# The residual of the second attention half added by TensorE, statistics and normalisation read from PSUM

## The chip, the cores and the metric

The kernel runs on one core of a Trainium2 chip. The metric is the device time of one execution in microseconds. Three runs of the kernel before gave 1319.53, 1314.14 and 1319.28 us, median 1319.28 us.

## The reference

A graph network with four layers runs over x of 1250 nodes by 512 features, with 40000 edges. Each layer first takes h = relu(layernorm(x)) and then adds its result to x. The change is in the second layer, an attention layer. Behind the attention itself, with o the attention's output after Wo, that layer computes:

```
x1 = layernorm(h + o) * ln1_g + ln1_b
f  = relu(x1 @ W1 + b1) @ W2 + b2          # 512 -> 256 -> 512
y  = layernorm(x1 + f) * ln2_g + ln2_b
x  = x + y
h  = relu(layernorm(x))                    # input of the third layer
M  = h @ Wm + bm                           # 512 -> 256, the third layer's messages
```

Only the step x1 + f and the statistics and normalisation that read it are changed. All arithmetic of this part is in 32-bit floats.

## The kernel before

The kernel is written by hand: each engine has its own instruction list, and semaphores order them. The nodes lie in ten tiles of 128 rows (the last has 98), and most stages are a loop over these tiles, spread over several engines. The order on each engine is the order of its list; nothing is rescheduled.

The stage that the change touches is called `l1b` in the code. Its work for tile t goes round like this.

- **TensorE** (`node_tiles`, L496 to L524). For tile t it writes one PSUM bank, t modulo 4. First comes a small 16-bit product with a row of ones, which lays down the bias (L511), and then two 32-bit products of 128 by 128 with 128 by 512 (L514). A 32-bit product is issued as two instructions, so L514 shows four MATMUL for a tile. From tile 4 on, it first waits until the bank's earlier tile is read (L504, semaphore `l1b_y`). After the product of tile t, from t = 6 on, it turns the tile t - 6 of the next layer's h with four transposes (L550, function `turn`), which wait until ScalarE has copied the turned tile two before out of PSUM. After the last tile, it computes the messages (L700, function `message`): eight MATMUL for a tile, four products in two instructions each. The first message waits for `l1b_y` of all ten tiles (L697), since the messages are written to banks 0 to 2, 4 and 5; for the weights `Wm` (L696), whose transfers SyncE issues once the products of all ten tiles are done (L374 to L377); and for the turned tile. Messages 0 to 3 run together behind turn 4, and then each turn is followed by one message, the last turn by two.
- **VectorE** (L1085 to L1104). In pass t it adds the residual to the bank and writes the sum to a buffer in SBUF (L1091, reading `H`, which holds x1), takes the statistics (L918, L919, L920), finishes mean and scale of the tile t - 1 (L925, L926), multiplies the normalised tile t - 2 with gamma (L1000), takes the statistics of the updated X of tile t - 3 (L918 to L920 again, reading X) and finishes the scale of tile t - 4 of X (L925, L926). A small instruction is followed by a wait for its own result where the next one reads it.
- **ScalarE** (`tail`, L1252 to L1267). In pass t: the square root of tile t (L1196), the normalisation of tile t - 1 in its SBUF buffer (L1242, semaphore `l1b_z`), the square root for X of tile t - 3, the relu of X of tile t - 4 into h (L1203), and the copy of the turned tile t - 6 out of PSUM (L1250).
- **GpSimd** (`shift_and_add`, L1372 to L1381). For each tile, it adds beta in the buffer (L1377) and adds the buffer to X (L1380).

The stage before it ends with the products of `x1 @ W1`, whose result ScalarE writes with a relu to SBUF (L1319). H of all ten tiles was complete before these products. Behind the messages VectorE adds their bias (L1109), and TensorE turns the edge-weight sums (L720) and goes on to the sums over edges (L736, L744).

Of the kernel before, what the change touches and what calls it, by code (L numbers as in the profile page):

```python
# [16 lines left out]
ACT = mybir.ActivationFunctionType  # L17
# [7 lines left out]
N, D, E = 1250, 512, 40000  # L25
T = -(-N // P)
KF = D // P
# [27 lines left out]
LAG = 6  # L55
# [41 lines left out]
def build(nc, A, out):  # L97
# [4 lines left out]
    with ExitStack() as ctx:  # L102
# [5 lines left out]
        def sem(name):  # L108
            if name not in sems:
                sems[name] = ctx.enter_context(nc.semaphore(name))  # L110
            return sems[name]
# [5 lines left out]
        H = sb("H", [P, T, D])  # L117
# [5 lines left out]
        stats = sb("stats", [P, 2, 6])  # L123
        mv = sb("mv", [P, 4, 2])
        rs = sb("rs", [P, 4, 2])
# [15 lines left out]
        PS = ctx.enter_context(nc.psum_tensor("PS", [P, 8 * BANK], F32))  # L141

        ident = K1[:, K_IDENT:K_IDENT + P]
# [9 lines left out]
        ybuf = R0[:, 0:4 * D].rearrange("p (s o) -> p s o", s=4)  # L153

        def bank(b, n=BANK):
            return PS[:, b * BANK:b * BANK + n]
# [55 lines left out]
        ybuf1 = R0[:, 5120:5120 + 4 * D].rearrange("p (s o) -> p s o", s=4)  # L212
# [19 lines left out]
        bias_parts = R0[0:BROWS, S0:S0 + D // 2].bitcast(BF16)  # L232
# [161 lines left out]
        def _(pe):  # L394
            mm = nc.tensor.matmul
# [98 lines left out]
                          "l0_h1_ps", "l0_h1_ev")  # L494

            def node_tiles(st, ks, lhs, rhs, width=D, turned=None, turned_width=KF, ready=None, then=None,  # L496
                           bias=None, banks=4, first=None, beside=None, lag=LAG, after=None):

                for t in range(T + (lag if turned else 0)):
                    if t < T:
                        if t >= banks:
                            pe.wait_ge(sem(st + "_y"), t - banks + 1)  # L504
                        if first:
                            first(t)
                        n = rows(t)
                        for part in range(len(ks)):
                            o = (t % banks) * BANK + part * width
                            if bias is not None:  # L510
                                mm(PS[0:n, o:o + width], ones_row[:, 0:n], bias, start=True, stop=False,  # L511
                                   skip_group_check=True)
                            for k in range(ks[part]):
                                i = mm(PS[0:n, o:o + width], lhs(part, k, t, n), rhs(part, k),  # L514
                                       start=k == 0 and bias is None, stop=k == ks[part] - 1, skip_group_check=True)
                        i.then_inc(sem(st + "_mm"), 1)
                        if beside:
                            beside(t)
                    if turned and t >= lag:
                        turn(st, t - lag, turned, turned_width, ready)  # L520
                    if then and t >= T:
                        then(t - lag)
                    if after and t > lag:
                        after(t - lag - 1)  # L524
# [167 lines left out]
            def message(t):  # L692

                n = rows(t)
                if t == 0:
                    pe.wait_ge(sem("l2_w_in"), 48)  # L696
                    pe.wait_ge(sem("l1b_y"), T)  # L697
                pe.wait_ge(sem("l1b_ht"), t + 1)
                for k in range(KF):
                    i = mm(PS[0:n, m_at(t):m_at(t) + 256], ht[:, k, t * P:t * P + n], wm[:, k, :], start=k == 0,  # L700
                           stop=k == KF - 1, skip_group_check=True)
                i.then_inc(sem("l2m_mm"), 1)

            def messages(i):
                for t in (range(0, i) if i == T - LAG else [i - 1]):
# [2 lines left out]

            pe.wait_ge(sem("l1_f1_ev"), 2)
            pe.wait_ge(sem("bias_parts"), BIAS_STEPS)  # L710
            node_tiles("l1b", [2], lambda q, k, t, n: f1t[:, k, t * P:t * P + n], lambda q, k: w2b[:, k, :],
                       turned=h_block, ready="l2_h", then=messages, bias=bias_parts)
            message(T - 1)

            def turn_sources(j, b0, done):
# [88 lines left out]
        def _(dve):  # L804
# [177 lines left out]
            def y_of(t, w=D, buf=ybuf):  # L982
                return buf[0:rows(t), t % 4, 0:w]
# [7 lines left out]
            def spread_of_y(name, t, w=D, buf=ybuf):  # L991
                spread_of(y_of(t, w, buf), rows(t), t % 4, name, stats, mv)
# [92 lines left out]
            for t in range(T + 4):  # L1085
                if t < T:
                    n = rows(t)
                    dve.wait_ge(sem("l1b_mm"), t + 1)
                    if t == 0:
                        dve.wait_ge(sem("l1_x1"), T)  # L1090
                    ve.tensor_tensor(y_of(t, D, ybuf1), bank(t % 4)[0:n], H[0:n, t, :], ALU.add).then_inc(sem("l1b_y"), 1)  # L1091
                    dve.wait_ge(sem("l1b_y"), t + 1)
                    spread_of_y("l1b_yn", t, D, ybuf1)
                if 1 <= t <= T:
                    scale_of_y("l1b_yn", t - 1)
                if 2 <= t < T + 2:
                    scaled("l1b", t - 2, bc1[:, 2, :], D, ybuf1)
                if 3 <= t < T + 3:
                    dve.wait_ge(sem("l1b_upd"), t - 2)
                    spread_of_x("l2_xn", t - 3)  # L1100
                if t >= 4:
                    scale_of_x("l2_xn", t - 4)
# [62 lines left out]
        def _(act):  # L1165
# [70 lines left out]
                for t in range((0, 3, 6, 9)[f], (3, 6, 9, T)[f]):  # L1236
                    lnc(t)

            def normed(st, t, w=D, buf=ybuf):
                n = rows(t)  # L1240
                act.wait_ge(sem(st + "_yn"), t + 1)
                sc.activation(buf[0:n, t % 4, 0:w], buf[0:n, t % 4, 0:w], ACT.Identity, bias=rs[0:n, t % 4, 1:2],  # L1242
                              scale=rs[0:n, t % 4, 0:1]).then_inc(sem(st + "_z"), 1)

            def turned(st, t, width=KF, dst=None):
# [3 lines left out]
                d = ht[:, :, t * P:t * P + n] if dst is None else dst[:, t * P:t * P + n]  # L1249
                sc.copy(d, src if dst is None else bank(6 + t % 2, n)).then_inc(sem(st + "_ht"), 1)  # L1250

            def tail(st, xn=None, done=None, width=KF, dst=None, w=D, buf=ybuf, beside=None, lag=LAG, after=None):  # L1252

                for t in range(T + lag + (1 if after else 0)):
                    if t < T:
                        root(st + "_yn", t, mv, rs)
                    if 1 <= t <= T:
                        normed(st, t - 1, w, buf)
                    if beside and t < T:
                        beside(t)  # L1260
                    if xn and 3 <= t < T + 3:
                        root(xn, t - 3, mv2, rs2)
                    if xn and 4 <= t < T + 4:
                        relu_rows(xn, done, rs2)(t - 4)
                    if lag <= t < T + lag:
                        turned(st, t - lag, width, dst)
                    if after and t > lag:  # L1267
                        after(t - lag - 1)
# [48 lines left out]
            for f in range(2):  # L1317
                act.wait_ge(sem("l1_f1_ps"), f + 1)
                sc.activation(f1t[:, f, 0:N], PS[:, 3 * f * BANK:3 * f * BANK + N], ACT.Relu,  # L1319
                              bias=bias_col[:, 4 + f:5 + f]).then_inc(sem("l1_f1_ev"), 1)  # L1320
            tail("l1b", "l2_xn", "l2_h", buf=ybuf1)


            act.wait_ge(sem("l1b_mm"), T)
# [129 lines left out]
```

## Time and profile before

| | |
|---|---|
| profiled execution | 1319.42 us |
| its span in the profile | 1317.2 us |
| median of three runs | 1319.28 us |
| TensorE matmul busy | 1155.9 us, 88% |
| VectorE busy | 630.0 us, 48% |
| ScalarE busy | 426.2 us, 32% |
| GpSimd busy | 142.6 us, 11% |
| granted TensorE clock, mean | 0.956 |

Times in the rows below are counted from the start of the span. Busy shares are means over stages that differ: the stage `l1b` with the messages behind it lies between 945.3 and 1002.0 us, and VectorE is busy in nearly all of its first 40 us. The granted clock is a share of the full 2.4 GHz; 0.50 is 1.2 GHz.

### The profile page before, as it was taken

To read this page: it belongs to the slowest core of one execution; us is meant where nothing else is said; L and a number is where in the kernel's file an instruction comes from. 1 tells how busy PE (TensorE), PEld (TensorE's weight loads), DVE (VectorE), ACT (ScalarE), POOL (GpSimd) and SP (SyncE) were. 2 spreads that over 40 slices of the span, in tenths; PEclk is the share of its full clock that TensorE was granted. 3 is DMA by queue.
4 is the path that set the end of the run, shared out by engine and by line. 5 is a ranking of instruction groups with operands and counts; after the bars stand their busy time and mean duration, and the time that the engine had idled before them with its cause. 6 is when DMAs were issued, how large, how long until landed. Compare 5 with 4: busy or idle time off the path is not lost.

```text
span 1317.2 us, 17306 instructions
## 1 busy us (share of the span) xinstructions
PE 1155.9 (88%) x5852; PEld 712.6 (54%) x5852; DVE 630.0 (48%) x1796; ACT 426.2 (32%) x711; POOL 142.6 (11%) x112
## 2 busy tenths in 40 slices
PE   1378877779999999979999999999868998799998
PEld 1134444445654445557777777764447556455543
DVE  6877877760007730056666666556394002610033
ACT  2401233320015440145555555543255003630000
POOL 0000000005560520000000000012172000200000
PEclk9997688779999999999999999999989999899999
DMA  4002477778783011000000000051010060000011
GB/s 145 0 0 59 132 199 211 202 203 298 257 271 124 0 32 48 17 1 1 1 2 1 2 1 1 1 187 75 0 33 0 0 227 0 1 32 0 0 40 38
DMA packets 67072, 93.78 MB, mean 71 GB/s; under 512 B 4857, under 2 KB 55872, under 8 KB 66998
## 3 DMA queue, kind: packets, MB, share of 16 engines
q1 hardware_dynamic: 66998, 92.78, 22.2%
q8 instruction: 48, 0.79, 0.3%
q14 instruction: 26, 0.21, 0.1%
HBM read 58.16 MB, written 34.60 MB: 70 GB/s over the span
## 4 chain that ended last, share of the span: by engine, by line
PE 71%; DVE 12%; DMA 7%; issue 4%; ACT 3%; SPq 2%; POOL 1%; DVEq 0%; ACTq 0%; POOLq 0%
PE PS L650 7%; PE PS L472 7%; PE PS L633 6%; PE PS L765 6%; PE PS L607 6%; PE PS L437 6%; DMA edge_parts<-X 6%; PE PS L514 5%; PE PS L799 5%; PE PS L578 5%; PE PS L736 3%; PE PS L744 3%; PE PS L487 3%; PE PS L568 2%; DVE R L1056 2%
## 5 line engine op out<-in xcount | busy, mean ns | idle before, releaser
L437 PE MATMUL PS<-HT,R 125*128 125x313 bf16 (+1 forms) x636 | 177.5, 414 | 64.0 <-DVE HT L947 26.4
L437 PEld LDWEIGHTS PS<-HT,R 125*128 x636 | 103.2, 172 | 139.0 <-issue 105.6
L1045 DVE CUSTOM_DVE_ANT_0 HT<-PS,CD 128x1250 f32<-128x1250 f32 (+1 forms) x80 | 116.4, 1455 | 55.4 <-issue 55.4
L633 PE MATMUL PS<-K,HT 128*128 128x128 f32 (+2 forms) x800 | 112.1, 279 | 15.3 <-DVE R L1056 14.5
L955 DVE TENSOR_SCALAR HT<-BC,HT 125x314 f16 x316 | 102.2, 365 | 35.7 <-PE PS L437 30.8
L1308 ACT ACTIVATE HT<-HT,soft 128x1250 f32<-128x1250 f32 (+1 forms) x80 | 107.1, 1339 | 19.7 <-DVE soft L1048 12.6
L1214 ACT COPY X<-PS 128x626 f32<-128x626 f32 x80 | 53.5, 689 | 170.2 <-PE PS L437 100.7
L633 PEld LDWEIGHTS PS<-K,HT 128*128 128x128 f32 (+2 forms) x800 | 83.8, 140 | 43.3 <-DVE R L1056 23.8
L1288 ACT COPY R<-PS 128x512 f32<-128x512 f32 (+1 forms) x120 | 64.8, 574 | 121.7 <-PE PS L633 119.8
L607 PE MATMUL PS<-R 64*128 64x512 f32 (+3 forms) x480 | 96.0, 532 | 4.8 <-DVE soft L1045 3.1
L650 PE MATMUL PS<-R 128*64 128x128 f32 (+2 forms) x1600 | 94.2, 273 | 0.0
L472 PE MATMUL PS<-CD,H 128*128 128x512 f32 (+2 forms) x240 | 87.5, 525 | 4.3 <-DMA CD<-edge_parts 4.3
L650 PEld LDWEIGHTS PS<-R 128*64 128x64 f32 (+1 forms) x1600 | 84.8, 137 | 6.4 <-issue 5.8
L765 PE MATMUL PS<-R,H 128*128 128x512 f32 (+2 forms) x240 | 85.5, 515 | 0.0
L1056 DVE COPY R<-PS 128x512 f32<-128x512 f32 (+1 forms) x80 | 54.3, 679 | 65.1 <-PE PS L633 65.1
L947 DVE TENSOR_SCALAR HT<-BC 125x314 bf16<-125x314 f16 x320 | 73.0, 301 | 13.8 <-PE PS L437 11.0
L607 PEld LDWEIGHTS PS<-R 64*128 64x128 f32 (+1 forms) x480 | 61.3, 185 | 32.2 <-issue 23.4
L1157 DVE SCALAR_TENSOR_TENSOR R<-PS,invdeg,BC 128x512 f32<-128x512 f32 (+1 forms) x10 | 7.5, 751 | 133.7 <-PE PS L799 133.7
L472 PEld LDWEIGHTS PS<-CD,H 128*128 128x128 f32 (+1 forms) x240 | 46.3, 195 | 44.5 <-issue 44.2
L578 PE MATMUL PS<-HT,R 128*128 128x512 f32 (+1 forms) x192 | 67.3, 513 | 0.0
L765 PEld LDWEIGHTS PS<-R,H 128*128 128x128 f32 (+1 forms) x240 | 45.3, 191 | 38.8 <-issue 38.7
L979 DVE TENSOR_SCALAR CD<-CD 128x1250 f32<-128x1250 f32 (+1 forms) x10 | 8.1, 807 | 99.6 <-ACT R L1228 99.5
(201 smaller groups left out, 1437.2 us busy)
## 6 DMA issues: line engine op xcount, KB each, us to landing
edge_parts<-X SPq DMA_DIRECT2D x160, 156.5 KB, 3.5
X<-edge_parts SPq DMA_DIRECT2D x15, 626.0 KB, 6.1
R<-edge_parts SPq DMA_DIRECT2D x15, 626.0 KB, 5.7
CD<-edge_sums SPq DMA_DIRECT2D x1, 6250.0 KB, 21.1
CD<-edge_parts SPq DMA_DIRECT2D x10, 469.5 KB, 4.4
CD<-edge_parts SPq DMA_DIRECT2D x3, 1565.0 KB, 10.9
X<-in_x SPq DMA_DIRECT2D x2, 2304.0 KB
edge_sums<-X SPq DMA_DIRECT2D x5, 625.0 KB, 5.4
```

The source lines that it names most:

```text
L437: return mm(bank(b0 + h, QUART), stat, hot, start=first, stop=True, skip_group_check=True)
L472: mm(bank(b0 + j, sn), H[0:rows(t), t, f * P:(f + 1) * P], cd[0:rows(t), t, s0:s0 + sn], start=t == 0, stop=t == T - 1, skip_group_check=True)
L578: i = mm(bank(3 * m + j, sn), wqk[p % 2][:, m, k, :], ht[:, k, s0:s0 + sn], start=k == 0, stop=k == KF - 1)
L607: i = mm(PS[0:n, a * N + s0:a * N + s0 + sn], qT[a * DK:(a + 1) * DK, p, t * P:t * P + n], kT[a * DK:(a + 1) * DK, p, s0:s0 + sn], start=T ...
L633: m = nc.tensor.transpose(PS[0:rows(j), o:o + n], Pb[u % 2][a][0:n, j * P:j * P + rows(j)], ident[0:n, 0:n])
L650: m = mm(PS[a * DK:(a + 1) * DK, o:o + n], V[0:rows(j), j, (2 * p + a) * DK:(2 * p + a + 1) * DK], PT[c % RING][0:rows(j), (2 * jj + a) * ...
L765: i = mm(bank(3 * (f % 2) + j, sn), H[0:rows(t), t, f * P:(f + 1) * P], cs[0:rows(t), t, s0:s0 + sn], start=t == 0, stop=t == T - 1)
L947: ve.tensor_scalar(src_oh[:, base_slot(w, q * GH + h), :], iota[0:EC, :], base_key[:, q, v:v + 1], None, ALU.is_equal).then_inc(sem("base_ ...
L955: i = ve.tensor_scalar(late_oh[:, bass.ds(m & (GEN - 1), 1), h, :].rearrange("p a n -> p (a n)"), iota[0:EC, :], key_base[0:EC, v:v + 1], ...
L1045: ve.tensor_tensor_reduce(Pb[s][a][0:n], PS[0:n, a * N:(a + 1) * N], cd[0:n, t, :], 1.0, -3e38, ALU.add, ALU.max, soft[0:n, s, a:a + 1]).t ...
L1056: ve.tensor_copy(PT[c % RING].rearrange("p (j n) -> p j n", j=4)[:, :, 0:n], bank(6 + c % 2).rearrange("p (j n) -> p j n", j=4)[:, :, 0:n])\
L1308: sc.activation(Pb[s][a][0:n], Pb[s][a][0:n], ACT.Exp, bias=soft[0:n, s, 2 + a:3 + a], accum_out=zsum[0:n, z + a:z + a + 1]).then_inc(sem( ...
```

## The change

TensorE adds the residual itself: between the bias and the two products of a tile stands one more 32-bit product, of the identity matrix with the tile of H, into the same bank. VectorE's addition (L1091) is gone, and its statistics read the bank. ScalarE's normalisation reads the bank and writes the SBUF buffer. The bank is therefore free only once the normalisation of its tile is done: the wait of tile t - 4 and the wait ahead of the first message go from `l1b_y` to `l1b_z`.

```diff
             def node_tiles(st, ks, lhs, rhs, width=D, turned=None, turned_width=KF, ready=None, then=None,
-                           bias=None, banks=4, first=None, beside=None, lag=LAG, after=None):
+                           bias=None, residual=None, banks=4, free="_y", first=None, beside=None, lag=LAG, after=None):
                 for t in range(T + (lag if turned else 0)):
                     if t < T:
                         if t >= banks:
-                            pe.wait_ge(sem(st + "_y"), t - banks + 1)
+                            pe.wait_ge(sem(st + free), t - banks + 1)
...
+                            if residual is not None:
+                                mm(PS[0:n, o:o + width], ident[0:n, 0:n], residual(t, n), start=False, stop=False,
+                                   skip_group_check=True)
...
                 if t == 0:
                     pe.wait_ge(sem("l2_w_in"), 48)
-                    pe.wait_ge(sem("l1b_y"), T)
+                    pe.wait_ge(sem("l1b_z"), T)
...
+            pe.wait_ge(sem("l1_x1"), T)
             node_tiles("l1b", [2], lambda q, k, t, n: f1t[:, k, t * P:t * P + n], lambda q, k: w2b[:, k, :],
-                       turned=h_block, ready="l2_h", then=messages, bias=bias_parts)
+                       turned=h_block, ready="l2_h", then=messages, bias=bias_parts,
+                       residual=lambda t, n: H[0:n, t, :], free="_z")
...
                     dve.wait_ge(sem("l1b_mm"), t + 1)
-                    if t == 0:
-                        dve.wait_ge(sem("l1_x1"), T)
-                    ve.tensor_tensor(y_of(t, D, ybuf1), bank(t % 4)[0:n], H[0:n, t, :], ALU.add).then_inc(sem("l1b_y"), 1)
-                    dve.wait_ge(sem("l1b_y"), t + 1)
-                    spread_of_y("l1b_yn", t, D, ybuf1)
+                    spread_of(bank(t % 4)[0:n], n, t % 4, "l1b_yn", stats, mv)
...
-            def normed(st, t, w=D, buf=ybuf):
+            def normed(st, t, w=D, buf=ybuf, from_psum=False):
                 n = rows(t)
                 act.wait_ge(sem(st + "_yn"), t + 1)
-                sc.activation(buf[0:n, t % 4, 0:w], buf[0:n, t % 4, 0:w], ACT.Identity, bias=rs[0:n, t % 4, 1:2],
+                src = bank(t % 4)[0:n] if from_psum else buf[0:n, t % 4, 0:w]
+                sc.activation(buf[0:n, t % 4, 0:w], src, ACT.Identity, bias=rs[0:n, t % 4, 1:2],
                               scale=rs[0:n, t % 4, 0:1]).then_inc(sem(st + "_z"), 1)
...
-            tail("l1b", "l2_xn", "l2_h", buf=ybuf1)
+            tail("l1b", "l2_xn", "l2_h", buf=ybuf1, from_psum=True)
```

## Rows read from the trace of the kernel before

**Rows 1.** The chain of waits, two pieces: start us, length us, engine and line.

```profile
949.42 0.70 DVE R L1091
992.67 0.81 ACT H L1203
```

**Rows 2.** Timeline of TensorE's products: start us, length us, instructions merged, idle before and releaser.

```profile
945.34 0.39 PE L511 MATMUL PS<-R 65*128 65x512 bf16 x1 [1.40 <-ACT R L1319]
945.56 1.88 PE L514 MATMUL PS<-WA,R 128*128 128x512 f32 x4
947.28 0.38 PE L511 MATMUL PS<-R 65*128 65x512 bf16 x1
...
963.28 1.11 PE L550 MATMUL PS<-K,H 128*128 128x128 f32 x4 [4.22 <-ACT H L1203]
...
972.45 1.88 PE L514 MATMUL PS<-WA,R 128*98 128x512 f32 x4
975.73 0.63 PE L550 MATMUL PS<-K,H 128*128 128x128 f32 x4 [1.40 <-ACT HT L1250]
979.68 1.09 PE L550 MATMUL PS<-K,H 128*128 128x128 f32 x4 [3.33 <-ACT HT L1250]
980.57 8.58 PE L700 MATMUL PS<-WA,HT 128*128 128x256 f32 x32
...
998.34 3.64 PE L700 MATMUL PS<-WA,HT 128*128 128x256 f32 x16
```

**Rows 3.** Timeline of VectorE in the same stage.

```profile
947.48 0.69 DVE L1091 TENSOR_TENSOR R<-PS,H 128x512 f32<-128x512 f32 x1 [21.53 <-PE PS L514]
...
955.95 0.87 DVE L926 SCALAR_TENSOR_TENSOR rs<-mv,rs 128x1 f32<-128x1 f32 x1
...
966.27 0.68 DVE L1091 TENSOR_TENSOR R<-PS,H 128x512 f32<-128x512 f32 x1
966.98 0.69 DVE L918 BATCH_NORM_STATS2 stats<-R 128x6 f32<-128x512 f32 x1
...
968.18 0.16 DVE L926 SCALAR_TENSOR_TENSOR rs<-mv,rs 128x1 f32<-128x1 f32 x1
968.26 0.68 DVE L1000 TENSOR_TENSOR R<-R 128x512 f32<-128x512 f32 x1
...
970.06 0.24 DVE L926 SCALAR_TENSOR_TENSOR rs<-mv,rs 128x1 f32<-128x1 f32 x1
970.23 0.68 DVE L1091 TENSOR_TENSOR R<-PS,H 128x512 f32<-128x512 f32 x1
...
982.29 1.24 DVE L926 SCALAR_TENSOR_TENSOR rs<-mv,rs 98x1 f32<-98x1 f32 x1
```

**Rows 4.** Timeline of GpSimd and ScalarE, pass 6 and the last normalisation.

```profile
969.02 1.26 POOL L1377 TENSOR_TENSOR R<-R 128x512 f32<-128x512 f32 x1 [1.34 <-DVE R L1000]
...
970.36 1.27 POOL L1380 TENSOR_TENSOR X<-X,R 128x512 f32<-128x512 f32 x1
...
983.56 0.81 ACT L1242 ACTIVATE R<-R,rs 98x512 f32<-98x512 f32 x1
```

**Rows 5.** Timeline of TensorE's weight loads, the one wait among the messages.

```profile
994.00 1.59 PEld L700 LDWEIGHTS PS<-WA,HT 128*128 128x128 f32 x8 [0.33 <-ACT HT L1250]
```

**Rows 6.** Busy time by stretch: us; PE, PEld, DVE, ACT, POOL; granted clock, DMA share, GB/s.

```profile
978.00:980.50 2.50, 0.81 (x4) 0.84 (x5) 2.36 (x8) 1.84 (x5) 1.47 (x2) 0.50 0.52 165
...
982.00:984.00 2.00, 2.00 (x7) 1.61 (x6) 1.97 (x4) 1.79 (x4) 1.44 (x2) 0.60 0.00 0
```

**Rows 7.** Timeline: the last issue of the third layer's weights by SyncE's queue.

```profile
975.33 0.50 SPq L377 DMA_DIRECT2D WA<-in_L_W  x1
```

**Rows 8.** DMA issues of 970 to 985 us: queue, count, KB each, us to landing.

```profile
WA<-in_L_W SPq DMA_DIRECT2D x2, 256.0 KB, 4.5
```

**Rows 9.** Groups by line, forms apart: count, busy us, mean ns of one.

```profile
L1056 DVE COPY R<-PS 128x512 f32<-128x512 f32 x72 | 49.8, 691 | 59.0 <-PE PS L633 59.0
L1347 ACT ACTIVATE R<-PS,valid 128x512 f32<-128x512 f32 x2 | 1.4, 689 | 0.0
```

More of the change, by code:

```diff
@@ L1250, in turned, with tail @@
                 sc.copy(d, src if dst is None else bank(6 + t % 2, n)).then_inc(sem(st + "_ht"), 1)
-            def tail(st, xn=None, done=None, width=KF, dst=None, w=D, buf=ybuf, beside=None, lag=LAG, after=None):
+            def tail(st, xn=None, done=None, width=KF, dst=None, w=D, buf=ybuf, beside=None, from_psum=False, lag=LAG, after=None):
                 for t in range(T + lag + (1 if after else 0)):
@@ L1257, in tail @@
                     if 1 <= t <= T:
-                        normed(st, t - 1, w, buf)
+                        normed(st, t - 1, w, buf, from_psum)
                     if beside and t < T:
```

## The prediction

> **What bounds the kernel now.** I read the chain of waits first. In this stage it runs on VectorE from 949.42 us, with small pieces of GpSimd, and comes back to TensorE by ScalarE's relu at 992.67 [rows 1]. The timelines show the rest. TensorE needs 1.94 us for a tile (945.34 to 947.28), VectorE a whole pass of 3.96 us (966.27 to 970.23), full without a gap [rows 2, 3]. So TensorE runs ahead and then waits (idle 4.22 us ahead of 963.28, 3.33 ahead of 979.68 [rows 2]). But from the first message at 980.57 to the end of the last at 998.34 + 3.64 = 1001.98, TensorE works through; its one wait there is 0.33 us [rows 2, 5]. The end of the stage hangs on two things that arrive nearly together: VectorE's chain, and the start of the first message. The chain of waits names only the first of them. The reader is to see that a gain on VectorE counts only if the first message also starts earlier.
>
> **TensorE, the added product.** The four instructions of L514 take 947.28 − 945.56 = 1.72 us from start to start, 0.43 each [rows 2]. The residual is one more 32-bit product of the same shape, two instructions, 0.86 us. A tile goes from 1.94 to 2.80 us, 8.6 us for ten tiles. It is on the path only at the start, where VectorE has nothing stored up. Before, the addition of tile 0 started at 947.48 [rows 3]. Now the statistics of tile t, up to tile 3, can start no earlier than 947.48 + 0.86 + 2.80 t: 948.34, 951.14, 953.94, 956.74.
>
> **VectorE, the removed addition.** In pass 6 it starts at 966.27 and the statistics at 966.98, so it is worth 0.71 us, and the bare pass is 3.96 − 0.71 = 3.25 us [rows 3]. Call s(t) the start of the gamma product L1000 in pass t; s(6) was 968.26. GpSimd's two additions then run from s + 0.76 to s + 2.02 and from s + 2.10 to s + 3.37 [rows 4]. They matter: the small L926 takes 0.16 us at 968.18, but 0.24, 0.87 and 1.24 us at 970.06, 955.95 and 982.29 [rows 3]; the first of these ends at 970.30, right behind GpSimd's 969.02 + 1.26 = 970.28 [rows 4]. The two exclude each other. In a steady pass only the second L926, at s + 1.80, met GpSimd. With the addition gone the next pass's first L926 would start at s + 3.17 and end at s + 3.33, and now meets the second GpSimd addition; it ends with that one, at about s + 3.38, and L1000 starts 0.08 before its end (968.18 + 0.16 against 968.26). The pass becomes 3.30 us, a saving of 0.66.
>
> Now in order. L1000 of pass 2 starts 1.28 us behind the statistics of tile 2 (966.98 to 968.26): s(2) = 953.94 + 1.28 = 955.22. In pass 3 the statistics start at 956.74, but L926 must wait for GpSimd's second addition, which ends at 955.22 + 3.37 = 958.59; s(3) = 958.52. Before, s(3) was 955.95 + 0.87 − 0.08 = 956.74: 1.8 us are lost to the slower first tiles. From there each pass takes 3.30 us: s(9) = 958.52 + 6 x 3.30 = 978.32. Before it was 968.26 + 3 x 3.96 = 980.14. So of ten removed additions, 7.1 us in name, 1.8 us are left at pass 9.
>
> Is TensorE late in between? Turn 0 needs h of tile 0, ready in pass 4; tile 8 is done at about 971.5, and VectorE asks for it at s(7) + 1.97 = 973.7. Tile 9 follows turn 2, which follows ScalarE's copy in pass 6. The same step for turn 4 came at 979.68, which is s(8) = 976.18 plus 3.50 [rows 2]. So turn 2 is at 968.42 + 3.50 = 971.92, and tile 9 ends 0.47 + 2.80 us later, at 975.2; VectorE asks for it at 977.0. The bank wait, now on the normalisation, is met: tile t needs the one of tile t − 4, which is done in pass t − 3, over two passes before. Behind that wait stand turn and next tile, with the same reserve.
>
> **The first message.** It now waits for the normalisation of tile 9. Before, that ran from 983.56 for 0.81 us [rows 4], 3.42 us behind s(9), because the last L926 stood 1.24 us behind GpSimd [rows 3]. The same order holds now: normalisation from 981.74 to 982.55, and with 0.14 us of signal (my estimate of the usual step between ScalarE's end and TensorE's start) the first message at 982.69. Before it started at 980.57, right behind turn 4. So it starts 2.1 us **later**, although VectorE is 1.8 us ahead. The weights are no longer late: their last issue came 975.33 − (972.45 + 1.88) = 1.00 us behind tile 9 and takes 4.5 us to land [rows 2, 7, 8], so they are there at 975.2 + 1.0 + 4.5 = 980.7.
>
> Behind the first message everything is queued on TensorE: messages, turns, then the turned edge weights and both sums. These wait for nothing else, since turned tiles and X come 1.8 us earlier than before; the 0.33 us wait [rows 5] goes.
>
> **TensorE's clock.** After an idle 1.40 us four transposes took 0.63 us, after 3.33 and 4.22 us 1.09 and 1.11 [rows 2]. The granted clock was 0.50 in 978 to 980.5 and 0.60 as the mean of 982 to 984, so 1.2 GHz up to about 983.6 [rows 6]: 3.0 us of the messages ran at half clock, which cost 1.5 us. Now TensorE idles about 3 us before the messages again (turn 4 at s(8) + 3.50 = 978.5 to 979.4, then the wait until 982.69). I expect the low clock again, for 3.0 to 3.9 us of the messages (3.9 is 979.68 to 983.6, from the first work to the rise). That costs 0 to 0.45 us more than before; I take 0.2. If the clock has stayed at 2.4 GHz, 1.5 us are won.
>
> **Reading PSUM instead of SBUF.** No row shows statistics of a bank. VectorE's copy of 128 by 512 from PSUM takes 691 ns [rows 9], statistics from SBUF 0.69 us [rows 3]. Lower end: no difference. Upper end: the addition's 0.71 us comes back in full. With x more for a tile, x under 0.05 is hidden under GpSimd; from there s(9) becomes 978.04 + 7x, 983.0 at the upper end, 4.7 us later. I take zero, by the copy, whose source and size are the same. The normalisation from PSUM lies between 0.69 (a ScalarE activation from PSUM with one pointer operand [rows 9]) and 0.81; it counts once, and I keep 0.81.
>
> The Trainium skill ("VectorE: DVE Perf Modes", the section on the TRN2 errata) gives VectorE a fixed cost of 120 cycles with a PSUM source and 58 with an SBUF one; as an estimate from this page x would be 0.065 us and the first message 0.2 us later still. The rows do not bear out such a difference: the copy from PSUM takes 691 ns, the product of two SBUF tiles 0.68 us [rows 3, 9]. By the rule the total would be 1321.6 in place of 1321.4.
>
> **The sum.** First message +2.1, the vanished wait −0.3, clock +0.2: +2.0 us. The profiled execution was 1319.42 us (span 1317.2, 2.2 outside), 0.14 above the median; 1321.4 us.
>
> **The rivals.**
> A, as worked out: 1321.4, own range 1320 to 1322.5. Chance 0.60.
> B, VectorE's chain is all that counts, as the chain of waits says: 10 x 0.71 = 7.1 us less, 1312.3. For it: the chain stays on VectorE until 992.67. Against it: the messages take 1001.98 − 980.57 = 21.4 us of TensorE in a row, so they would have to start near 973.5, before tile 9 is even through, and the weights allow 980.7. Chance 0.07.
> C, statistics from a bank are dear. At the upper end the first message comes 4.7 us later still: +2.0 + 4.7 = +6.7, 1326.1, slower than before. It begins to decide at x = 0.05. Against it stands the copy's 691 ns. Chance 0.12.
> D, the clock. TensorE is busier in the stage, 2.80 us instead of 1.94 for a tile, and could enter the messages at full clock: 1321.4 − 1.7 = 1319.7. Against it: the two idle stretches from 975.7 on, each near 3 us. If the normalisation is also cheaper, or the last L926 slips in before GpSimd, the message starts at the weights' 980.7 and the sum is 0.1 − 0.3 − 1.5 = −1.7, 1317.7. Chance 0.21.
>
> A measurement of this kernel can tell 0.5%, 6.6 us, from no change. Only B goes below −6.6, and only the end of C with a long low clock above +6.6. The range reaches from 1315 (below D, since one of three runs was 5.1 us under the median) to 1325. Faster 0.07, same 0.88, slower 0.05.
>
> **What would show it.** Statistics L918 of tiles 0 to 3 at a rhythm of 2.80 us; then passes of 3.30 us, with both L926 of a pass ending with a GpSimd addition; L1242 of tile 9 near 981.7; the first message right behind it, near 982.7, and no longer behind turn 4; granted clock 0.50 at its start; the last message's end near 1004. It would be wrong if L918 on a bank took over 0.75 us, if the first message started before 981, or if VectorE's pass were not 3.2 to 3.4 us.

## The result: 0.23% slower, as forecast

Over 22 runs of each kernel the changed one took 1321.93 us (median), the kernel before 1319.03 us: ratio 1.0023, 95% interval 1.0013 to 1.0033, or 1.7 to 4.4 us slower. The forecast was 1321.4 us, 2.0 us slower, with a range of 1315 to 1325. The profiled execution of the changed kernel took 1321.26 us (span 1319.3).

The part before the stage differs by some us from one execution to the next whatever the kernel, so places in the stage are compared by their distance from its first product (945.34 us before, 946.13 after), in one profiled execution of each kernel. By that measure the first message starts at 35.23 us before and 37.34 after, 2.11 later, and the last message ends at 56.64 and 59.30, 2.66 later. Nearly all of the 2.9 us lies here.

TensorE's timeline after the change, in the columns of [rows 2] (L514 is now the added product, L517 the two products, L553 the transposes, L703 the messages):

```profile
946.13 0.39 PE L511 MATMUL PS<-R 65*128 65x512 bf16 x1 [1.40 <-ACT R L1321]
946.35 1.02 PE L514 MATMUL PS<-H,K 128*128 128x512 f32 x2
947.22 1.88 PE L517 MATMUL PS<-WA,R 128*128 128x512 f32 x4
948.93 0.38 PE L511 MATMUL PS<-R 65*128 65x512 bf16 x1
...
974.30 1.88 PE L517 MATMUL PS<-WA,R 128*98 128x512 f32 x4
976.07 0.63 PE L553 MATMUL PS<-K,H 128*128 128x128 f32 x4
979.38 0.63 PE L553 MATMUL PS<-K,H 128*128 128x128 f32 x4 [2.68 <-ACT HT L1252]
983.47 9.48 PE L703 MATMUL PS<-WA,HT 128*128 128x256 f32 x32 [3.46 <-issue]
...
1001.79 3.64 PE L703 MATMUL PS<-WA,HT 128*128 128x256 f32 x16
```

A tile takes 2.80 us (946.13 to 948.93) against 1.94 [rows 2]. The messages no longer stand right behind turn 4 but 3.46 us of idle time later, and the first four take 9.48 us against 8.58.

VectorE's timeline, the first encounter with GpSimd and one steady pass, to be laid beside [rows 3]:

```profile
958.72 0.67 DVE L931 SCALAR_TENSOR_TENSOR rs<-mv,rs 128x1 f32<-128x1 f32 x1
...
965.78 0.23 DVE L931 SCALAR_TENSOR_TENSOR rs<-mv,rs 128x1 f32<-128x1 f32 x1
965.94 0.68 DVE L1005 TENSOR_TENSOR R<-R 128x512 f32<-128x512 f32 x1
...
967.73 0.25 DVE L931 SCALAR_TENSOR_TENSOR rs<-mv,rs 128x1 f32<-128x1 f32 x1
967.90 0.69 DVE L923 BATCH_NORM_STATS2 stats<-PS 128x6 f32<-128x512 f32 x1
...
969.10 0.23 DVE L931 SCALAR_TENSOR_TENSOR rs<-mv,rs 128x1 f32<-128x1 f32 x1
969.25 0.68 DVE L1005 TENSOR_TENSOR R<-R 128x512 f32<-128x512 f32 x1
```

The pass is 969.25 − 965.94 = 3.31 us. Both L931 of a pass now last 0.23 to 0.25 us, where one lasted 0.16 before.

The groups of the statistics by what they read (count, busy us, mean ns):

```profile
L923 DVE BATCH_NORM_STATS2 stats<-X 128x6 f32<-128x512 f32 x27 | 18.6, 688 | 2.6 <-POOL X L1382 2.3
L923 DVE BATCH_NORM_STATS2 stats<-PS 128x6 f32<-128x512 f32 x9 | 6.2, 691 | 28.0 <-PE PS L517 28.0
```

The last scale of the stage on VectorE, then ScalarE's copy of turn 3 and its last normalisation:

```profile
981.32 1.23 DVE L931 SCALAR_TENSOR_TENSOR rs<-mv,rs 98x1 f32<-98x1 f32 x1
...
981.97 0.56 ACT L1252 COPY HT<-PS 128x512 f32<-128x512 f32 x1
982.59 0.78 ACT L1244 ACTIVATE R<-PS,rs 98x512 f32<-98x512 f32 x1
```

The granted clock by stretch (columns as in [rows 6]):

```profile
978.00:980.50 2.50, 0.63 (x4) 0.42 (x4) 2.36 (x8) 2.07 (x4) 1.80 (x2) 1.00 1.01 322
980.50:982.00 1.50, 0.00 (x0) 0.00 (x0) 1.40 (x6) 0.95 (x3) 1.42 (x2) 0.79 0.33 113
982.00:984.00 2.00, 0.53 (x1) 0.50 (x2) 1.94 (x4) 1.31 (x3) 1.30 (x2) 0.50 0.00 0
984.00:986.00 2.00, 2.00 (x6) 1.61 (x5) 1.07 (x4) 1.49 (x3) 1.92 (x2) 0.50 0.00 0
986.00:988.00 2.00, 2.00 (x6) 1.55 (x6) 1.26 (x5) 0.52 (x2) 1.92 (x3) 0.50 0.00 0
988.00:990.00 2.00, 2.00 (x11) 1.74 (x10) 1.07 (x4) 0.50 (x1) 1.94 (x4) 0.95 0.00 0
```

The normalisation ends at 982.59 + 0.78 = 983.37, and the first message starts at 983.47. The chain of waits tells it otherwise:

```profile
976.63 0.51 SPq L376
977.14 0.04 issue
977.19 4.69 DMA WA<-in_L_W
981.88 1.59 issue
983.47 0.77 PE PS L703
```

It puts the wait down to the weights' transfer and calls the last 1.59 us "issue". The transfer had landed 1.59 us before. The first message has three waits (weights, normalisations, turned tile), and the chain names only the one that it could see; e1 below tests which of them held it.

### The profile page after: what moved, and what is told of

It reads as the page before. It is cut to its first block, busy times and chain, and to the rows that moved or that the text cites. A ratio compares the mean times of both kernels' runs of the same rounds, so it can differ in the third digit from the quotient of the medians.

```text
span 1319.3 us, 17335 instructions
## 1 busy us (share of the span) xinstructions
PE 1163.3 (88%) x5872; PEld 714.2 (54%) x5872; DVE 624.1 (47%) x1786; ACT 426.0 (32%) x711; POOL 142.6 (11%) x112
## 4 chain that ended last, share of the span: by engine, by line
PE 72%; DVE 11%; DMA 7%; issue 4%; ACT 4%; SPq 1%; DVEq 0%; POOLq 0%; POOL 0%; ACTq 0%
PE PS L653 7%; PE PS L472 7%; PE PS L636 6%; PE PS L770 6%; PE PS L437 6%; DMA edge_parts<-X 6%; PE PS L610 6%; PE PS L517 5%; PE PS L804 5%; PE PS L581 5%; PE PS L741 3%; PE PS L749 3%; PE PS L487 3%; PE PS L571 3%; DVE R L1061 2%
```

## The experiments

Each ran in twelve executions, beside as many or more of the kernel before on the same chip; ratios are to that. The interval of an experiment is 2.9 to 4.2 us wide, and every ratio lies within 0.4% of 1, so the verdicts rest on the profiles, one for each kernel. The two columns in the middle are us from the first product of the stage.

| kernel | first message | last message ends | ratio to before (interval) |
|---|---|---|---|
| before | 35.23 | 56.64 | 1 |
| changed | 37.34 | 59.30 | 1.0023 (1.0013 to 1.0033) |
| e1 wait moved | 36.20 | 57.96 | 1.0016 (1.0002 to 1.0029) |
| e2 no product | 34.41 | 55.66 | 0.9985 (0.9974 to 0.9996) |
| e3 product alone | 38.24 | 59.54 | 1.0026 (1.0015 to 1.0037) |
| e4 one input | 36.80 | 59.08 | 1.0017 (1.0003 to 1.0030) |
| e5 filled | 38.83 | 58.38 | 1.0008 (0.9995 to 1.0021) |
| e6 early weights | 33.70 | 54.94 | 0.9991 (0.9978 to 1.0004) |
| e7 interleaved | 27.00 | 55.35 | 1.0003 (0.9987 to 1.0019) |
| e8 before, one input | 35.35 | 55.83 | 1.0015 (1.0001 to 1.0029) |
| e9 filled both | 37.37 | 56.99 | 1.0012 (0.9998 to 1.0027) |
| e10 messages ahead | 30.41 | 54.90 | 0.9992 (0.9979 to 1.0004) |
| e11 ahead, one input | 30.12 | 53.06 | 0.9969 (0.9954 to 0.9984) |

**e1, the wait moved.** To the changed kernel:

```diff
                     pe.wait_ge(sem("l2_w_in"), 48)
+                if t == 4:
                     pe.wait_ge(sem("l1b_z"), T)
```

> The changed kernel with one edit: the wait for the normalisation of all ten tiles stands ahead of message 4 (the first that writes a bank of the stage) and no longer ahead of message 0, which writes bank 4. Theory (the first message waits for the normalisation of tile 9): it now starts when the weights are there, about 36 us behind the first bias product of the stage against 37.3 in the changed kernel and 35.2 before; the last message ends 1.3 to 2.3 us earlier than in the changed kernel, and the whole is 1.5 to 2 us faster than it. Rival (the weights' transfer released it, as the chain of waits names it): no change, first message at 37.3. Rival (VectorE's chain sets the stage's end): no change in the end either.

The chain of waits, the same columns as above:

```profile
980.74 5.09 DMA WA<-in_L_W
985.83 0.04 issue
985.87 9.28 PE PS L704 x32
```

The first message now starts 0.04 us behind the landing, at 36.20, 1.14 earlier than in the changed kernel, and the last message ends 1.34 earlier. Nothing else was touched, so in the changed kernel the normalisation was what it waited for, and the transfer is the next in line. Both rivals fall. The whole was forecast 1.5 to 2 us faster than the changed kernel; the two ratios differ by 0.9 us, which their intervals can't tell from nothing.

**e2, the product left out.** To the changed kernel; the residual is missing from the sum:

```diff
-                            if residual is not None:
-                                mm(PS[0:n, o:o + width], ident[0:n, 0:n], residual(t, n), start=False, stop=False,
-                                   skip_group_check=True)
```

> The changed kernel without the added product: the residual is left out of the sum, VectorE's addition is gone and statistics and normalisation read the bank. Theory: VectorE runs passes of 3.30 us from the start on, the normalisation of tile 9 is done 2.5 us earlier than in the changed kernel, the first message starts about 34.8 us behind the stage's first product (35.2 before), and the whole is within 0.5 to 1 us of the kernel before, though all ten additions are gone. Rival (VectorE's chain is the path, 0.71 us a tile): 6 to 7 us faster than before.

```profile
983.02 8.77 PE L700 MATMUL PS<-WA,HT 128*128 128x256 f32 x32 [3.46 <-issue]
```

First message at 34.41 (34.8 expected), end 0.98 us earlier than before, the whole 0.5 to 3.4 us faster. Ten additions of 0.71 us are gone for nothing in return, and the stage wins one microsecond: TensorE still waits 3.46 us ahead of the first message, which starts 0.09 us behind the end of the last normalisation (982.93). Rival B of the prediction, VectorE's chain as the whole path, would have given 6 to 7.

**e3, the product alone.** To the kernel before, in `node_tiles` (with `residual` as a parameter, handed in as in the change); the bias product starts the bank anew:

```diff
                             o = (t % banks) * BANK + part * width
+                            if residual is not None:
+                                mm(PS[0:n, o:o + width], ident[0:n, 0:n], residual(t, n), start=True, stop=False,
+                                   skip_group_check=True)
```

> The kernel before plus the added product alone, put ahead of the bias product, which overwrites it; VectorE still adds the residual. Theory: the first tiles come 2.80 us apart, VectorE enters its steady rhythm of 3.96 us about 2.5 us later and never catches up; first message about 38 us behind the stage's first product (35.2 before), the whole 2.5 to 3.3 us slower than before. Rival (the product is hidden except in tile 0, since TensorE waits later): 0.9 us slower.

```profile
988.34 8.82 PE L703 MATMUL PS<-WA,HT 128*128 128x256 f32 x32 [0.62 <-DMA WA<-in_L_W]
```

First message at 38.24 (38 expected), end 2.90 us later than before, the whole 2.0 to 4.9 us slower. Turn 4 comes 2.65 us later than before (36.99 against 34.34), which is the price of the slower first tiles; ahead of the first message stand 0.62 us more, for the weights, which are issued behind tile 9 and so come later too. Removing the additions then gives back 0.24 us at the end of the stage (59.54 to 59.30): most of what VectorE wins goes to the new wait and the clock.

**e4, one SBUF input.** To the changed kernel, for all stages:

```diff
-                ve.scalar_tensor_tensor(r[0:n, slot, 1:2], m[0:n, slot, 0:1], -1.0, r[0:n, slot, 0:1], ALU.mult,
-                                        ALU.mult).then_inc(sem(name), 1)
+                ve.tensor_scalar(r[0:n, slot, 1:2], m[0:n, slot, 0:1], r[0:n, slot, 0:1], -1.0, ALU.mult,
+                                 ALU.mult).then_inc(sem(name), 1)
```

> The changed kernel with the small VectorE instruction that writes -mean times scale (L926 of before, L931 now) made a tensor_scalar with the scale as pointer operand: one SBUF tensor input in place of two, in every stage. Theory (two SBUF inputs exclude GpSimd): none of them lasts over 0.2 us; a pass takes 3.25 us in place of 3.31; the last one no longer stands 1.2 us behind GpSimd, so that the first message starts 1.5 to 2.3 us earlier; with the same in other stages the whole is 2 to 5 us faster than the changed kernel. Rival (any VectorE instruction that writes here waits for GpSimd): the same durations of 0.25 to 1.2 us and no gain.

Groups by line, and the rows of one pass with GpSimd:

```profile
L931 DVE TENSOR_SCALAR rs<-mv,rs 128x1 f32<-128x1 f32 x63 | 13.5, 214 | 2.2
```

```profile
966.86 1.27 POOL L1379 TENSOR_TENSOR R<-R 128x512 f32<-128x512 f32 x1 [0.63 <-DVE R L1005]
...
967.89 0.21 DVE L931 TENSOR_SCALAR rs<-mv,rs 128x1 f32<-128x1 f32 x1
...
968.20 1.27 POOL L1382 TENSOR_TENSOR X<-X,R 128x512 f32<-128x512 f32 x1
...
969.23 0.21 DVE L931 TENSOR_SCALAR rs<-mv,rs 128x1 f32<-128x1 f32 x1
969.36 0.68 DVE L1005 TENSOR_TENSOR R<-R 128x512 f32<-128x512 f32 x1
```

None of these small instructions waits any more: 0.21 us each, also while GpSimd runs (966.86 to 968.13). With two SBUF inputs the instruction excluded GpSimd's addition, with one input and a pointer it doesn't. But much of the wait only moves on. The gamma product behind it also reads two SBUF tiles, and now it is the one that meets GpSimd:

```profile
984.49 1.26 POOL L1382 TENSOR_TENSOR X<-X,R 128x512 f32<-128x512 f32 x1
...
984.63 1.66 DVE L1005 TENSOR_TENSOR R<-R 128x512 f32<-128x512 f32 x1
```

Over the whole kernel the small instructions are busy 4.0 us less than in the changed kernel, and the gamma products (L1005) 2.7 us more (the largest group has a mean of 829 ns in place of 681). The first message came only 0.54 us earlier, not 1.5 to 2.3. The scale of tile 9 was ready at 984.50 + 0.21 = 984.71, but ScalarE's list had the relu of tile 5 and the copy of turn 3 ahead of the normalisation, which started at 985.62 and ended at 986.40. I had counted VectorE's wait and left out the list behind it: in the changed kernel, too, ScalarE's copy ended at 982.53, level with the scale at 982.55. The whole, forecast 2 to 5 us faster than the changed kernel, was 0.8 us faster by the ratios, which is within the noise.

**e8, the same in the kernel before.** The diff of e4, to the kernel before.

> The kernel before with only the small VectorE instruction L926 changed to one SBUF tensor input, in all stages. Theory: no L926 lasts over 0.22 us, but each is 0.05 us longer than the undisturbed 0.16; the first message is set by turn 4 and moves by under 0.7 us, so the whole is 0 to 2 us faster than before. Rival (the waits on GpSimd are worth their sum on the path): 4 us or more.

```profile
986.85 8.00 PE L700 MATMUL PS<-WA,HT 128*128 128x256 f32 x32
```

The stage ends 0.81 us earlier, yet the whole was 0.1 to 3.9 us slower than before, where 0 to 2 us faster was expected: a miss. The stage's gain isn't the instruction's alone. The first message starts 0.12 us later than before; 0.58 us of the gain is that messages 0 to 3 took 8.00 us in place of 8.58, because less of them ran at the low clock, and the rest that the 0.33 us wait among the messages is gone. And as in e4 the wait moves on: the small instructions are busy 3.4 us less than before, the gamma products (L1000) 2.5 us more. That explains why little is gained, not why anything is lost; what the instruction is worth over the whole stays open.

**e5, TensorE's idle time filled.** To the changed kernel:

```diff
                 if t == 0:
+                    for _ in range(4):
+                        mm(bank(4), ident, H[:, 0, :], start=True, stop=True, skip_group_check=True)
                     pe.wait_ge(sem("l2_w_in"), 48)
```

> The changed kernel with four more products of the identity with a tile of H, written to bank 4 (which message 0 overwrites), between turn 4 and the first message's waits: 3.4 us of work in TensorE's idle time, nothing waits for it. Theory (TensorE idles 3.5 us while it waits for the normalisation, and its clock falls to 1.2 GHz for the messages): the granted clock stays at 1.00, the first message starts at the same 37.3 us behind the stage's first product, messages 0 to 3 take 6.9 to 7.1 us in place of 9.48, and the stage ends 2.3 to 2.5 us earlier than in the changed kernel. Rival (the messages are slow by themselves): 9.5 us again and no gain.

```profile
988.64 5.29 PE L700 MATMUL PS<-H,K 128*128 128x512 f32 x8
993.77 7.07 PE L705 MATMUL PS<-WA,HT 128*128 128x256 f32 x32
```

The four messages took 7.07 us, so they aren't slow by themselves. But the filling took 5.1 us in place of 3.4 and made the first message 1.5 us late: the clock had fallen during the filling (0.50 in 990 to 992). The idle 2.68 us ahead of turn 4 was still there, and e9 tests whether that was the reason. The stage ends 0.92 us earlier than in the changed kernel, not 2.3 to 2.5.

**e9, both idle stretches filled.** As e5, with three products in place of four, and three more behind turn 3:

```diff
+                    if st == "l1b" and t == T - 1:
+                        for _ in range(3):
+                            mm(bank(4), ident, H[:, 0, :], start=True, stop=True, skip_group_check=True)
```

> The changed kernel with three products of the identity with a tile of H behind turn 3 and three behind turn 4, written to bank 4, which message 0 overwrites; each set fits into TensorE's idle stretch there (2.7 and 3.5 us). In the run with four behind turn 4 alone the clock had already fallen at the third. Theory (the idle stretches take the clock down): the granted clock stays at 1.00 throughout, the first message starts 37.3 us behind the stage's first product (as in the changed kernel), messages 0 to 3 take 6.9 to 7.1 us, and the last message ends 56.7 to 57.0 us behind it (59.3 changed, 56.6 before). Rival (the clock falls whatever stands there): messages 0 to 3 over 8 us, end at 58 or later.

```profile
987.83 7.14 PE L708 MATMUL PS<-WA,HT 128*128 128x256 f32 x32 [0.91 <-issue]
```

```profile
980.00:984.00 4.00, 3.90 (x15) 1.76 (x14) 3.76 (x14) 3.02 (x8) 2.81 (x3) 1.00 0.60 146
984.00:988.00 4.00, 3.10 (x11) 1.34 (x9) 3.86 (x10) 2.68 (x5) 2.94 (x3) 1.00 0.38 121
988.00:992.00 4.00, 4.00 (x19) 3.51 (x19) 2.62 (x11) 1.69 (x4) 3.84 (x4) 1.00 0.00 0
```

The clock stays at 1.00, the first message starts where it did (37.37), and the end comes 2.31 us earlier than in the changed kernel, at 56.99. So the low clock cost the changed kernel 2.3 us in the profiled execution, and its idle stretches, not the work, brought it down. The first of them is enough for that: in e5 and in e6 below the second is gone, and the clock fell all the same. The second alone wasn't tried. The added products compute nothing that is used.

**e6, early weights.** As e1, and the weights of the messages in a transfer of their own, issued when their place is free:

```diff
+            sp.wait_ge(sem("l1_f1_ps"), 2)
+            sp.dma_start(wm, A["L2_Wm"].rearrange("(k p) o -> p k o", p=P)).then_inc(sem("l2_wm_in"), 16)
             sp.wait_ge(sem("l1b_mm"), T)
-            sp.dma_start(wm, A["L2_Wm"].rearrange("(k p) o -> p k o", p=P)).then_inc(sem("l2_w_in"), 16)
...
-                    pe.wait_ge(sem("l2_w_in"), 48)
-                    pe.wait_ge(sem("l1b_z"), T)
+                    pe.wait_ge(sem("l2_wm_in"), 16)
+                if t == 4:
+                    pe.wait_ge(sem("l1b_z"), T)
...
             pe.wait_ge(sem("o1_ev"), 2)
+            pe.wait_ge(sem("l2_w_in"), 32)
```

> The changed kernel with the wait for the normalisations ahead of message 4 and the message weights loaded as soon as their place is free, before the stage. Theory (first message set by these two in turn): it starts right behind turn 4, 33.7 us behind the stage's first product, the last message ends 54.4 to 55.3 us behind it (56.6 before, 59.3 changed), and the whole is 1.3 to 2.3 us faster than the kernel before. Rival (VectorE's and ScalarE's chain of tile 9 then ends later than the messages): end at 57 or later.

First message at 33.70, end at 54.94, both as worked out: with both waits out of the way turn 4 sets the start again. Messages 0 to 3 took 8.76 us, so part of them still ran at the low clock, with only the 2.68 us of idle time ahead of turn 4. The whole is 1.2 us faster than before, with an interval that reaches 0.5 us to the other side.

**e7, messages in the idle time, VectorE still adding.** To the kernel before, the edits of e6 (with `l1b_y`) and e4, and:

```diff
+                    if between and lag + 2 <= t < T:
+                        between(t - lag - 2)
...
-                for t in (range(0, i) if i == T - LAG else [i - 1]):
+                for t in (range(2, i) if i == T - LAG else [i - 1]):
...
-                       turned=h_block, ready="l2_h", then=messages, bias=bias_parts)
+                       turned=h_block, ready="l2_h", then=messages, bias=bias_parts, between=message)
```

> The kernel before (VectorE adds the residual) with the weights loaded early, messages 0 and 1 put behind turns 2 and 3 in TensorE's idle time, messages 2 and 3 behind turn 4, the bank wait ahead of message 4, and the small VectorE instruction with one SBUF tensor input in all stages. Theory: the last message ends 52.5 to 54 us behind the stage's first product (56.6 before); with the small instruction the whole is 3 to 5 us faster than before. Rival (tile 9's chain through GpSimd, VectorE and ScalarE ends last anyway): end at 56 or later, whole within 1.5 us of before.

```profile
991.43 2.00 PE L702 MATMUL PS<-WA,HT 128*128 128x256 f32 x8 [1.53 <-ACT HT L1253]
...
994.75 1.97 PE L702 MATMUL PS<-WA,HT 128*128 128x256 f32 x8 [0.90 <-ACT HT L1253]
...
997.84 1.99 PE L702 MATMUL PS<-WA,HT 128*128 128x256 f32 x8 [0.68 <-ACT HT L1253]
```

End at 55.35, where 52.5 to 54 was expected: TensorE has less to do behind the first message and now waits for ScalarE's copies, which follow VectorE's passes. The whole, forecast 3 to 5 us faster than before, wasn't faster at all (1.7 us faster to 2.5 slower), as the rival had it. Part of it is the clock again: message 0, behind turn 2, took 2.83 us at the low clock. With VectorE adding, this order brought nothing that can be measured.

**e10 and e11, messages in the idle time, TensorE adding.** To e6, for e10, and with e4's edit besides for e11:

```diff
+                    if between and t == T - 1:
+                        between(0)
+                        between(1)
...
-                for t in (range(0, i) if i == T - LAG else [i - 1]):
+                for t in (range(2, i) if i == T - LAG else [i - 1]):
...
-                       residual=lambda t, n: H[0:n, t, :], free="_z")
+                       residual=lambda t, n: H[0:n, t, :], free="_z", between=message)
```

> The changed kernel with the weights loaded early, messages 0 and 1 behind turn 3, in TensorE's idle stretch, messages 2 and 3 behind turn 4, and the wait for the normalisations ahead of message 4. Theory: TensorE's work behind the first message no longer sets the end; tile 9's chain does, and it is about 1.8 us ahead of that of the kernel before by the removed additions: the last message ends 53.3 to 54.8 us behind the stage's first product (54.9 with early weights alone, 55.4 with the same order and VectorE adding), the whole 2 to 3.5 us faster than before. Rival (ScalarE's list, which copies the turned tiles between the relus, sets the pace): 55 or later.

> The same with the small VectorE instruction with one SBUF tensor input, in all stages. Theory: tile 9's scale no longer stands 1.6 us behind GpSimd's split of the next bias; the last message ends 0.3 to 1.3 us earlier than without it. Over the whole I expect within 1 us of the kernel without it: the instruction is 0.05 us longer each of 70 times and saves waits that mostly lie off the path. Rival: it gains its full 4 us of waits.

e10 ends at 54.90, no better than e6 and just outside the forecast (53.3 to 54.8), although the granted clock stayed at 1.00 through its messages. The whole was 1.1 us faster than before (2.8 faster to 0.5 slower), where 2 to 3.5 was expected. Its two last scales on VectorE, the first of them 1.58 us long, since it stands behind GpSimd's split of the next bias:

```profile
994.67 1.58 DVE L935 SCALAR_TENSOR_TENSOR rs<-mv,rs 128x1 f32<-128x1 f32 x1
...
996.36 0.56 DVE L935 SCALAR_TENSOR_TENSOR rs<-mv,rs 98x1 f32<-98x1 f32 x1
```

```profile
997.62 1.99 PE L706 MATMUL PS<-WA,HT 128*128 128x256 f32 x8 [1.56 <-ACT HT L1256]
```

TensorE waits 1.56 us for what follows it. Without this conflict, e11 ends at 53.06, 1.84 us earlier than e10, where 0.3 to 1.3 was expected, and 3.58 earlier than the kernel before. Its whole is faster than before by 0.31%, 2.1 to 6.1 us, and 2.5 us faster than e10 by the medians (1318.90 against 1321.41), where less than 1 us was expected: that is a second miss on what the small instruction is worth over the whole, on the other side from e8. By their ratios to the kernel before, e11 beats the changed kernel as well. It keeps the change under study, but that the change is part of the gain isn't shown: the same order of messages with VectorE adding wasn't run, and e7, the nearest to it, has messages 0 and 1 in other places.

## Why the prediction was right

Point by point:

- **The added product:** 2.80 us a tile forecast, 2.80 measured. e3 shows its price by itself: 2.65 us at turn 4, 2.90 us at the end of the stage, where the weights come late as well.
- **VectorE's pass:** 3.30 us forecast, 3.31 measured. The second meeting with GpSimd is there (0.23 us in place of 0.16), and so is the one in pass 3 (0.67 us at 958.72), which made VectorE start its steady passes late.
- **Reading a bank:** x was taken as zero; statistics took 691 ns from a bank and 688 from X. Rival C falls. (By its own sum, 978.04 + 7x against 978.32, the threshold of x was 0.04 us, not 0.05; nothing hangs on it.) The fixed costs of the Trainium skill ("VectorE: DVE Perf Modes", the section on the TRN2 errata), from which x was estimated at 0.065 us, aren't borne out for this instruction.
- **The first message:** +2.1 us forecast, +2.11 measured, and right behind the normalisation. e1 shows that this wait held it. It was the step most easily left out, since before the change the wait in its place, for the additions, cost nothing. One reason given for its size was half of the truth: the last L926 did stand 1.24 us behind GpSimd, but ScalarE's copy ahead of the normalisation ended as late as that scale, at 983.50 against 983.53 before and at 982.53 against 982.55 after. That the old distance of 3.42 us carried over was right either way.
- **The wait among the messages:** 0.33 us gone, as forecast.
- **The clock:** the one term that was mis-sized. I forecast a low clock over 3.0 to 3.9 us of the messages, at 0 to 0.45 us, and took 0.2. It was low up to about 988.2, 4.7 us of the messages, and these took 0.90 us longer than before. The clock was still at 1.00 at turn 4 and fell only near 981.4 (0.79 as the mean of 980.5 to 982); before, it had fallen ahead of turn 4, and it rose sooner. But the change doesn't fix when the clock falls. e2 has the changed kernel's two idle stretches (2.67 and 3.46 us), and its messages took 8.77 us in place of 9.48; e8 has the work of the kernel before and its idle time ahead of turn 4 (3.35 us against 3.33), and took 8.00 in place of 8.58. So with one profile of each kernel, how much of the 0.90 us belongs to the change and how much to the execution stays open. Rival D, that it would stay high, is what e9 produced by hand.

The sum of what was measured: 2.11 + 0.90 − 0.35 = 2.66 us in the stage, the last term being what the vanished wait leaves. That this agrees with the whole's 2.9 us to a few tenths is more than the interval can vouch for, and so is the distance of only half a microsecond between the forecast 1321.4 and the median: the mechanism is shown by the places in the stage, not by that.

Rival B, 7.1 us faster, fell with the result, and e2 shows why: the chain of waits followed VectorE, but the first message's start was nearly as late.

## What to carry to other kernels

When work moves from a busy engine to an idle one, look at who waits for whom at both ends of the stage: here the idle engine was on the path for the first four tiles, and a wait that had been free became the last one. Look at what a wait protects, too: the first four messages wrote banks that the stage does not use, so the wait stood four messages too early. A small instruction with two SBUF inputs next to a busy GpSimd can last nearly eight times as long as alone (1.24 us against 0.16), but freeing it helps only if the next instruction doesn't take over the wait and the engine behind it isn't just as late.

## What the runs showed of the hardware that I had not expected

TensorE's clock fell although a burst of four transposes (0.63 us) stood between two idle stretches of 2.68 and 3.46 us, and it fell after the burst. With the second of the two stretches filled it still fell (e5), with both filled it didn't (e9). How much of the messages ran at 1.2 GHz differed from kernel to kernel and wasn't set by the order of idle time and work alone: 3.0 us before and 4.7 after the change, but 1.9 in e8, whose stage is that of before but for the small instruction, and 3.3 in e2, with the same idle stretches as after.

A one-column VectorE instruction on two SBUF inputs lasted up to 1.59 us when GpSimd was in the middle of an addition; the same arithmetic with one input and a pointer operand took 0.21 us in e4 (mean of all 70: 214 ns). The next instruction with two SBUF inputs then took the wait over: the gamma product at 984.63 lasted 1.66 us in place of 0.68.
